# A fused adapter and expert-LoRA kernel: the order of its start-up loads and transposes, one buffer for W, and the order of copies at the end of a sum

## The reference

```python
# x: (8, 512, 2048); A0: (64, 2048, 16); B0: (64, 16, 2048); ids, lang: (8,)
# W: (2048, 2048); Wr: (8, 2048); A: (8, 16, 2048); Bm: (8, 2048, 16)
x = x + einsum('bnr,bor->bno', einsum('bni,bri->bnr', x, B0[ids]), A0[ids])
base = einsum('btd,od->bto', x, W)
logits = einsum('btd,ed->bte', x, Wr) + one_hot(lang, 8)[:, None, :] * 5.0
topw, topi = top_k(logits, 2)
gates = sum(one_hot(topi, 8) * softmax(topw)[..., None], -2)
h = einsum('btd,erd->bter', x, A)
out = x + base + 2.0 * einsum('bter,bte,eor->bto', h, gates, Bm)
```

## Time and profile before

| | |
|---|---|
| median of 3 runs | 1612.02 us (1610.12 to 1613.25) |
| the profiled execution | 1612.52 us, span 1610.7 us |
| TensorE busy | 1582.4 us (98%), 7762 matmuls |
| VectorE busy | 1180.0 us (73%) |
| ScalarE busy | 754.2 us (47%) |
| POOL busy | 74.9 us (5%) |
| granted clock, mean | 0.993 |
| DMA | 351.45 MB, mean 218 GB/s |

### The profile page before, as it was taken

The page is one execution under the profiler, slowest core; times in us unless marked ns, Lnnn a source line. Parts: engine busy times, 40 slices in busy tenths (PEclk is TensorE's granted clock), DMA queues, the critical chain, the costliest instruction groups (busy, mean ns, idle before and its releaser), DMA issues.

```text
span 1610.7 us, 21189 instructions
## 1 busy us (share of the span) xinstructions
PE 1582.4 (98%) x7762; PEld 1337.3 (83%) x7762; DVE 1180.0 (73%) x1603; ACT 754.2 (47%) x988; POOL 74.9 (5%) x117
## 2 busy tenths in 40 slices
PE   8789999999999999999999999999999999999998
PEld 8678888788888888888888888888888888888887
DVE  5674444787678876987768976888769877787665
ACT  6444343254444554454444544445444544445443
POOL 1222222200000000000000000000000000000000
PEclk9899999999999999999999999999999999999999
DMA  9878687869787897779876897879977788576664
GB/s 266 220 231 249 191 248 205 226 199 234 197 227 228 218 214 206 232 214 238 205 219 219 218 232 184 236 230 228 213 199 233 220 228 200 199 232 202 208 221 159
DMA packets 375514, 351.45 MB, mean 218 GB/s; under 512 B 250538, under 2 KB 294874, under 8 KB 374362
## 3 DMA queue, kind: packets, MB, share of 16 engines
q1 hardware_dynamic: 366146, 318.62, 71.8%
q0 software_dynamic: 8992, 30.94, 6.1%
q10 hardware_dynamic: 272, 0.52, 0.1%
HBM read 280.75 MB, written 68.82 MB: 217 GB/s over the span
## 4 chain that ended last, share of the span: by engine, by line
PE 94%; DMA 2%; DVE 1%; SPq 1%; issue 1%; ACT 1%; POOL 0%; ACTq 0%; DVEq 0%; POOLq 0%
PE pb L779 27%; PE pb L780 27%; PE pb L781 27%; PE pb L388 4%; PE pb L390 3%; PE pb L542 2%; PE pb L682 1%; DMA raw<-in_L_cond_W_dram 1%; PE pb L321 1%; SPq L658 0%; DMA b0n<-in_L_cond_B_dram 0%; DMA t_scr<-tst 0%; PE pb L957 0%; PE pb L424 0%; SPq L1311 0%
## 5 line engine op out<-in xcount | busy, mean ns | idle before, releaser
L775 DVE TENSOR_TENSOR wl<-raw,wh 128x1024 fp32r<-128x1024 f32 (+1 forms) x456 | 555.2, 1218 | 333.5 <-ACT wh L771 333.3
L771 ACT CAST wh<-raw 128x1024 fp32r<-128x1024 f32 (+1 forms) x456 | 477.0, 1046 | 687.7 <-PE pb L781 683.4
L779 PE MATMUL pb<-wh,sh 128*128 128x512 f32 x1568 | 613.5, 391 | 0.5 <-DVE ost L815 0.5
L780 PE MATMUL pb<-wl,sh 128*128 128x512 f32 x1568 | 612.3, 390 | 0.0
L781 PE MATMUL pb<-wh,sl 128*128 128x512 f32 x1568 | 611.8, 390 | 0.0
L781 PEld LDWEIGHTS pb<-wh,sl 128*128 128x128 f32 x1568 | 294.5, 188 | 62.6
L779 PEld LDWEIGHTS pb<-wh,sh 128*128 128x128 f32 x1568 | 294.9, 188 | 56.0 <-DVE wl L775 0.9
L780 PEld LDWEIGHTS pb<-wl,sh 128*128 128x128 f32 x1568 | 294.9, 188 | 54.7
L388 PE MATMUL pb<-awb,xah 128*128 128x304 f32 x512 | 138.5, 304 | 0.0
L390 PE MATMUL pb<-awb,xal 128*128 128x256 f32 x512 | 134.5, 280 | 0.0
L779 PE MATMUL pb<-wh,xh 128*128 128x512 f32 x256 | 106.3, 415 | 3.9 <-DVE xl L569 3.1
(11 more groups left out here) (144 smaller groups left out, 1339.8 us busy)
## 6 DMA issues: line engine op xcount, KB each, us to landing
raw<-t_scr SPq DMA_DIRECT2D x392, 512.0 KB, 4.3
xst<-in_x_dram SPq DMA_DIRECT2D x768, 32.0 KB, 3.8
raw<-in_L_cond_W_dram SPq DMA_DIRECT2D x128, 128.0 KB, 4.0
t_scr<-tst POOLq DMA_DIRECT2D x32, 512.0 KB, 5.0
raw<-bt_scr SPq DMA_DIRECT2D x28, 512.0 KB, 3.8
out_dram<-ost SPq DMA_DIRECT2D x28, 512.0 KB, 4.4
out_dram<-u SPq DMA_DIRECT2D x28, 512.0 KB, 3.4
t_scr<-raw POOLq DMA_DIRECT2D x32, 256.0 KB, 5.1
```

The lines of the kernel that those rows point to most:

```text
L771: e.copy(pair_split(wh, g), pair_source(g)).then_inc(c_wh, 1)
L775: e.tensor_tensor(out=pair_split(wl, g), in0=pair_source(g), in1=pair_split(wh, g).bitcast(f32), op=ALU.subtract).then_inc(c_wl, 1)
L779: e.matmul(o, h, wh[:, g % RING, k, :], start=start, stop=False)
L780: e.matmul(o, h, wl[:, g % RING, k, :], start=False, stop=False)
```

## The change

- A is loaded in two halves with a semaphore each (`d_a[0]`, `d_a[1]`); the second is issued after x load 1, and groups 2 and 3 of A are transposed in steps 0 and 1. Four more warm-up transposes stand behind the first two units of x.
- A0 is loaded ahead of B0, x loads 4, 5 and 6 between its parts, x load 7 between the parts of B0. A0's groups are transposed in steps 5 to 8 (banks 2 and 3) and 11 to 14 (banks 4 and 5), B0's in 9 to 12; `a0_rows` in steps 9 and 10 in place of 11 and 12. The second half of the aux product is in banks 0 and 1.
- Pair 2 of W is loaded into wrn, with a semaphore of its own, as soon as wrn is transposed; pairs 3 to 7 take the other of the two places than before, pair 3 needs pair 0's, pair 4 pair 1's, pair 8 pair 7's, pair 9 pair 6's.
- On SP bn and the stores to a_scr stand ahead of pair 3, the stores to b0_scr behind it. On POOL `w_store(0)` stands behind the arrival of bn and four of the copies to bnj, the other four are ahead of `w_sums_store(0)`.
- `g_products` is cut at 7, 11, 16; deltas 2 and 3 and their splits stand ahead of half 1 of pair 1; `g_sum` stands behind the splits, `g_lo` behind `pair_lo(1)`.
- In slot 6 delta unit 15 is adapted and split ahead of the split of pair 8; in each ninth slot `first_evacuate` stands ahead of the split of the next pair, on both engines, and on ScalarE also ahead of x_keep and x_hi.

```diff
+        def raw_place(g):
+            return (g + 1) % 2 if 3 <= g < 8 else g % 2
         def w_raw(g):
-            return raw[:, g % 2, :, :]...
+            place = wrn[:, 0:2 * CW] if g == 2 else raw[:, raw_place(g), :, :]...
         def first_load(e, g):
-            if g >= 2:
-                if (g - 2) % 9 == 8:
-                    e.wait_ge(c_wl, g - 1)
-                else:
-                    e.wait_ge(c_wt, 2 * w_number(g - 2) + 2)
+            if g == 2:
+                e.wait_ge(c_ap, 3)
+            elif g == 9:
+                e.wait_ge(c_wt, 2 * w_number(6) + 2)
+            elif g >= 3:
+                before = {3: 0, 4: 1, 8: 7}.get(g, g - 2)
+                if before % 9 == 8:
+                    e.wait_ge(c_wl, before + 1)
+                else:
+                    e.wait_ge(c_wt, 2 * w_number(before) + 2)
...
         def pe_start(e):
-            warm(e)
+            warm(e, 18)
             for u in range(2):
                 x_transpose(e, 0, u)
+            warm(e, 4)
             for m in range(2):
                 a_transpose(e, m)
             small_transpose(e)
-            for m in range(2, 4):
-                a_transpose(e, m)
...
-                if 3 <= s < 7:
-                    b0_transpose(e, s - 3)
-                if 7 <= s < 15:
+                if s < 2:
+                    a_transpose(e, 2 + s)
+                if 5 <= s < 9:
+                    a0_transpose(e, s - 5)
+                if 9 <= s < 13:
+                    b0_transpose(e, s - 9)
+                if 11 <= s < 15:
                     a0_transpose(e, s - 7)
...
-            g_products(e, range(12, 16))
-            w_transpose(e, 1, 1)
+            g_products(e, range(11, 16))
             for u in range(2, 4):
                 delta(e, 0, u)
+            w_transpose(e, 1, 1)
             w_transpose(e, 2, 0)
...
         def dve_start(e):
...
-            g_sum(e)
             for u in range(2, 4):
                 adapt(e, 0, u)
             for u in range(2, 4):
                 first_lo(e, u)
+            g_sum(e)
+            pair_lo(e, 1)
             g_lo(e)
-            pair_lo(e, 1)
...
         def pool_start(e):
-            w_store(e, 0)
+            e.wait_ge(d_bn, 16)
+            for m in range(E):
+                if m == 4:
+                    w_store(e, 0)
+                e.tensor_copy(bnj[...], bn[:, m, :, :]).then_inc(c_bnj, 1)
             w_sums_store(e, 0)
             w_store(e, 1)
-            e.wait_ge(d_bn, 16)
-            for m in range(E):
-                e.tensor_copy(bnj[...], bn[:, m, :, :]).then_inc(c_bnj, 1)
...
         def sp_start(e):
-            e.dma_start(an[:, :], A...).then_inc(d_a, 16)
+            e.dma_start(an[:, 0:HO], rows[:, 0:HO]).then_inc(d_a[0], 16)
...
+            x_load(e, 0, 1)
+            e.dma_start(an[:, HO:D], rows[:, HO:D]).then_inc(d_a[1], 16)
+            for m in range(2, 4):
                 x_load(e, 0, m)
+            for b in range(1, NB):
+                adapter.append(e.value_load(ids[0:1, b:b + 1], ...))
+                a0_load(b)
+                if b % 2:
+                    if b < 7:
+                        x_load(e, 0, 4 + b // 2)
+                    else:
+                        a0_load(0)
+            for b in range(4):
+                b0_load(b)
+            x_load(e, 0, 7)
+            for b in range(4, NB):
+                b0_load(b)
...
-            for g in range(2):
+            for g in range(3):
                 first_load(e, g)
-            e.wait_ge(c_bpl, 4)
-            for s, t in enumerate((b0h, b0l)):
-                e.dma_start(b0_scr[:, :, s, :], t[:, :, :]).then_inc(d_b0s, 16)
             e.wait_ge(c_ar, 2)
...
+            e.wait_ge(c_tr, 16)
+            e.dma_start(bn, Bm...).then_inc(d_bn, 16)
             for s, t in enumerate((arh, arl)):
                 e.dma_start(a_scr[s, :, 0:D], t).then_inc(d_as, 16)
-            first_load(e, 2)
             first_load(e, 3)
-            e.dma_start(bn, Bm...).then_inc(d_bn, 16)
+            e.wait_ge(c_bpl, 4)
+            for s, t in enumerate((b0h, b0l)):
+                e.dma_start(b0_scr[:, :, s, :], t[:, :, :]).then_inc(d_b0s, 16)
             first_load(e, 4)
...
         def dve_main(e):
             for i in range(SLOTS0):
+                if i == 6:
+                    adapt(e, 0, 15)
+                    first_lo(e, 15)
+                if i % 9 == 8:
+                    for t in (0, 2):
+                        first_evacuate(e, i // 9, t)
                 pair_lo(e, i + 2)
...
-                if i % 9 == 8:
-                    for t in (0, 2):
-                        first_evacuate(e, i // 9, t)
```

More of the change, by code:

```diff
@@ L368, in aux_bank @@
         def aux_bank(n, half):
-            return 2 if n == 0 and half else 4
+            return 0 if n == 0 and half else 4
         def aux_products(e, n, u):
@@ L951, in adapted_moe_lora_kernel, with warm @@
         G_ROWS = ((0, 0), (R, 0), (2 * R, 1))
-        def warm(e):
+        def warm(e, n):
             e.wait_ge(c_pool, 3)
-            for m in range(18):
+            for m in range(n):
                 e.transpose(pb[:, 4, m % 4 * P:(m % 4 + 1) * P], ident[:, :], ident[:, :])
         def a_transpose(e, m):
-            if m == 0:
-                e.wait_ge(d_a, 16)
+            if m % 2 == 0:
+                e.wait_ge(d_a[m // 2], 16)
             for k in range(4):
@@ L1030, in a0_transpose @@
                 block = a0p[:, at, :, :].rearrange("p b r -> p (b r)") if g < 4 else a0t[:, at * P:(at + 1) * P]
-                last = e.transpose(pb[:, g % 2, m * P:(m + 1) * P], block, ident[:, :])
+                last = e.transpose(pb[:, a0_bank(g), m * P:(m + 1) * P], block, ident[:, :])
             last.then_inc(c_at, 1)
@@ L1208, in dve_start @@
             small_lo(e)
-            for m in range(2, 4):
-                a_lo(e, m)
             x_keep_dve(e, 3)
@@ L1394, in act_main @@
                     w_keep(e, i + 2, 1)
+                if i == 6:
+                    first_hi(e, 15)
+                if i % 9 == 8:
+                    if more:
+                        w_keep(e, i + 3, 0)
+                    for t in (1, 3):
+                        first_evacuate(e, i // 9, t)
                 pair_hi(e, i + 2)
@@ L1403, in act_main @@
                     x_keep(e, 1, i - 9)
-                if more:
+                if i % 9 != 8 and more:
                     w_keep(e, i + 3, 0)
@@ L1407, in act_main @@
                     bt_copy(e, 2 * i - 1)
-                for u in DELTAS0.get(i, ()):
-                    first_hi(e, u)
+                if i < 6:
+                    for u in DELTAS0[i]:
+                        first_hi(e, u)
                 if 9 <= i < 25:
@@ L1460, in dve_main @@
                     top_two(e, 0)
-                for u in DELTAS0.get(i, ()):
-                    adapt(e, 0, u)
-                for u in DELTAS0.get(i, ()):
-                    first_lo(e, u)
+                if i < 6:
+                    for u in DELTAS0[i]:
+                        adapt(e, 0, u)
+                    for u in DELTAS0[i]:
+                        first_lo(e, u)
                 if i == 29:
```

110 lines of the change are left out of this document (58 added, 52 removed).

## The result

The changed kernel is slower: 1623.97 us (four runs, 1623.03 to 1625.06) against 1612.62 for the kernel before with the runs added since; ratio 1.0074, 95% interval 1.0056 to 1.0091. The profiled execution took 1623.03 us with a span of 1621.2, 10.5 us over the span before.

The account below looks back on a forecast made before the run. TensorE was taken as the bound, busy 98% of the span, its largest wait 8.4 us on a load of W. Gains of 5.3 + 0.8 + 4.4 + 0.5 = 11.0 us from 1612.5 gave 1601.5 us, range 1594 to 1609.

Parts of the forecast that it names:

- Copies of sums first: Slots 18 and 27: TensorE's 1.3 us of waits for ost shrink, x_keep comes later; gain 0.5 us, ends -0.5 and 1.3.
- Pair 2 in wrn: Start of W's products: the 8.4 us wait for W goes, products start at 59.3 instead of 64.54; gain 5.3 us.
- Pair 4 later still: nothing: Loads of W behind pair 2: pair 4 is wanted later than pair 3, covered by twelve products; no gain or loss.
- Rival 4: SP's queue: pair 4's load, behind stores and copies, lands at 85 and becomes the wait; 1618.7 us, chance 0.07.
- The front: Loads and transposes of A, A0, B0: shorter wait for A, limited by A0's arrival; gain 0.8 us, ends -2.5 and +3.
- rival 5: Start: TensorE reaches A0's transposes too soon, stands over 3 us, clock falls; 2.5 us lost, 1609 us, chance 0.12.
- the cap by A0: A0's transposes: a0p, there only at about 25.5, leaves 0.6 to 1 of the 6 us from A's earlier landing.
- Slot 6: Last delta unit first, pair 9's load sooner: 3.1 us wait becomes 1.1, clock holds; gain 4.4 us, ends 0.6 and 6.
- rival 2: No gain at slot 6: bt_scr's stores set the landing of the sums; only 0.6 of 4.4 left, 1605.3 us, chance 0.20.
- Rival 3: VectorE's adapt and split chain: POOL's eight bnj copies block it 0.4 us each, 3.2 us; 1603.8 us, chance 0.10.

Follow-up runs that it names:

- the kernel with the columns moved: The changed kernel without the sums first, with SP's load of the adapter's columns (awb from b0_scr) moved behind pair 5's load: 1611.24 us, 0.9997 of the kernel before.
- the b0_scr run: The changed kernel without the sums first, with SP's two stores to b0_scr moved behind pair 4's load: 1613.73 us, 1.0024 of the kernel before.

## Why the prediction was wrong

The forecast was 1601.5 us, 11 us faster; it came out 11.4 us slower. The step on the copies of sums did most of that, but it is not the only one: without it the kernel stands at 1613.45 us, where the other terms of the sum give 1602.0. By its own steps:

- **Copies of sums first, +0.5 us forecast.** This is the step that failed: it cost 9.9 us in the trace, 12.4 alone, and taking it out of the change gave 10.5 back. The step looked at who waits for the copies (1.3 us of ost) and at x_keep, one instruction behind them on ScalarE. The copies themselves wait, for the end of the gated products, and in the kernel before they stood last in their slot so that nothing had to wait with them. The step also named pair_hi, behind the copies on ScalarE, but priced only its length and not the copies' wait. The prediction didn't list what is behind them on VectorE (pair_lo, w_sums, add_identity, bx_lo) and who waits for each. All of it was in the code and none in the earlier trace rows, as a wait that doesn't exist yet has no row. x_keep, which it did name, costs 0.6 us at 206.6, close to its 0.7.
- **Pair 2 in wrn, 5.3 us forecast.** The wait for W went and `w_keep(2, 0)` took its place, released by the store of pair 0, as written (2.07 us of wait for t_scr); the copy ran at 60.70 where 57.5 was taken, products at 62.46 and not 59.3, 2.1 us gained. The term mis-sized is bn: issued at 41.91 where 40.3 was reckoned, and copied by POOL from 52.23 on, not 47.8, 10.3 us from issue and not 7.5. The low clock was to stay as long as before; it lasts 6.8 us where it was 10.2, and 0.7 us more are gained by pair 3. One wait was missed, without cost: the first half of pair 2 (57.49) waits 3.0 us for `w_keep(1, 1)`, now behind first_hi(3).
- **"Pair 4 later still: nothing."** True for pair 4, wrong for pair 5, which the step didn't follow: 4.3 us lost. Rival 4 had the mechanism (SP's loads behind the stores to b0_scr) one pair too early and at a rate too low (the DMA moved 373 GB/s in 50 to 60, where the rival took 157); the missing piece was awb's load from b0_scr right ahead of pair 5.
- **The front, +0.8 forecast.** a0p was reckoned for 25.5 and came at 25.45, TensorE started on it at 25.50. But the range end of 2.5 us of loss was nearer than the middle: TensorE came 3.6 us early, stood, and its clock fell after it. It is 1.35 us behind at pair 0; across the six kernels with this front it was between 0.8 ahead and 3.4 behind. The wait for A did go, but one of 1.55 us for a load of x (12.04) came, which the step had not. This is rival 5, and the cap by A0 was right.
- **Slot 6, 4.4 forecast, 0.5 measured.** Both premises failed. Pair 9's load left earlier, but w_sums(7) could go on only 6.8 us after the store of the sums of pair 6 was issued (106.24 to 113.01), where it was 7.4 in the kernel before (104.76 to 112.16): 0.6 us gained and not 1.4, close to rival 2. And on ScalarE unit 15 now stands ahead of `w_keep(9, 0)`, so TensorE waits 3.35 us for that in place of 3.1 for xl. The step named what unit 15 no longer stands behind and not what stands behind unit 15.
- **Rival 3, the shared port.** The splits at 53.32 took 1.69 us for two where two took 1.29, 0.4 us once, not eight times. The first of them began with POOL's fourth copy, but the second (0.88 us) lay beside POOL's stores of pair 0 and no copy, so that the copies held them up isn't shown; and this chain wasn't the bound.

The range ended at 1609. The prediction gave the slower side 6 in 100, on one rival alone, and no rival for the ninth slots. Its sums are right but for the chance of faster, which is 0.87 by its own parts and not 0.86.

## What to carry to other kernels

Before an instruction is moved ahead, ask what it waits for, and list everything it now holds back on its engine, to the end of the slot and into the next: a copy that waits for TensorE belongs last. A place made free for one load gains only if the loads behind it in the queue come sooner too; here 7 us at pair 2 were worth 0.4 us until pair 3 and bn stood ahead of the stores as well. And letting TensorE reach a late load sooner gained nothing in this front: it stood 3.6 us for A0 there, and paid for the clock besides.

## What the runs showed of the hardware

The wait of 3.2 us at pair 5 (81.55), in the middle of full work, goes with a granted clock of 0.83 over 80 to 90, that is, in part at the lower of its two levels, and 4.3 us were lost where 3.2 were waited; the wait of 2.2 us for pair 32 cost 2.4 us and no more. A wait can cost more than its length. Issuing a load is not free behind others: four loads of 128 KB took SP 9.7 us right behind two 1 MB stores, 5.06 us right behind 256 KB in small pieces, and 2.0 us at 72.13 in the kernel with the columns moved. Executions of one kernel differ by up to 8 us here (1610.5 to 1618.8 for the b0_scr run, 1610.0 to 1616.5 for the change without sums first); that this comes from the race between loads and TensorE at the front is a guess, as only one execution of each has a trace. The execution with the trace lay 5.8 us from the median in the run with the sums first alone; the jumps at one place repeat far better than the sum.
